# Modulation rows spread by DMA and copied into PSUM by ScalarE, in a fused residual stack on one core

## The reference, cut to what matters

```python
ctx = causal_ema(x, tau_ctx)
wg = sigmoid(concat([x, ctx]) @ Wg.T + bg)
gated = x * wg
h1 = gelu(x @ Wn1.T + bn1)
mod = 0.5 + sigmoid(h1 @ Wn2.T + bn2)            # [b, t, 16]
# for each of the 16 values of d:
traces[d] = causal_ema(gated * mod[..., d], tau_raws[d])
temporal = sum_d traces[d] * softmax(blend)[d]
gate = sigmoid(temporal @ Wtemp.T + btemp)
soma = gelu(x @ Wsoma.T + bsoma)
x = x + layernorm((soma * gate) @ Wout.T)
```

## Time and profile before

| | before |
|---|---|
| median of 3 runs | 2875.97 us |
| lowest, highest | 2873.36, 2878.23 us |
| profiled execution | 2876.17 us |
| its span, first to last instruction | 2874.4 us |
| granted TensorE clock, mean | 0.993 |
| busy: TensorE, VectorE, ScalarE, GpSimd | 2818.4, 1846.4, 1390.2, 1233.3 us |
| moved by DMA | 201.22 MB |

### The profile page before, as it was taken

One profiled execution on the slowest core, in us unless ns is written; L12 is line 12 of the kernel. 1 busy time (PEld: TensorE's weight loads), 2 busy tenths in 40 slices (PEclk: granted clock), 3 DMA queues, 4 the chain that ended last, 5 costly groups with the idle time before them and its releaser, 6 DMA issues.

```text
span 2874.4 us, 36550 instructions
## 1 busy us (share of the span) xinstructions
PE 2818.4 (98%) x13018; PEld 2331.4 (81%) x13018; DVE 1846.4 (64%) x3017; ACT 1390.2 (48%) x2408; POOL 1233.3 (43%) x950
## 2 busy tenths in 40 slices
PE   8699999999999999999999999999999999999999
PEld 5488888788888888888788888888888888888888
DVE  8699778867777766556865666655776563333443
ACT  4544555465336633454534553344643473333445
POOL 5256434643463445433554345542455333333333
PEclk9899999999999999999999999999999999999999
DMA  4133332322112311111311131111221122111231
GB/s 150 60 116 99 90 94 78 111 92 93 57 48 68 115 48 50 48 50 48 94 45 48 56 92 45 48 45 52 74 70 57 47 87 63 50 45 44 72 92 57
DMA packets 85573, 201.22 MB, mean 70 GB/s; under 512 B 10312, under 2 KB 27152, under 8 KB 85392
## 3 DMA queue, kind: packets, MB, share of 16 engines
q1 hardware_dynamic: 82256, 190.38, 21.5%
q0 software_dynamic: 2560, 8.39, 1.0%
q10 hardware_dynamic: 576, 0.11, 0.0%
HBM read 190.75 MB, written 8.09 MB: 69 GB/s over the span
## 4 chain that ended last, share of the span: by engine, by line
PE 88%; DVE 7%; issue 2%; ACT 2%; DMA 1%; SPq 0%; DVEq 0%; ACTq 0%
PE bank L557 19%; PE bank L559 19%; PE bank L558 19%; PE ps_out L557 9%; PE ps_out L559 9%; PE ps_out L558 9%; DVE trace L1075 2%; DVE w_lo L1145 2%; DVE trace L1067 1%; PE bank L550 1%; PE bank L631 1%; DVE hid L1169 0%; DMA stat<-mod_rows 0%; ACT L867 0%; PE bank L679 0%
## 5 line engine op out<-in xcount | busy, mean ns | idle before, releaser
L1308 POOL TENSOR_TENSOR hid_lo<-hid,hid_hi 128x512 fp32r<-128x512 f32 x640 | 865.6, 1353 | 1581.2 <-ACT hid_hi L954 1580.9
L557 PE MATMUL bank<-res_lo,w_hi 128*128 128x512 f32 x2432 | 963.3, 396 | 6.2 <-DVE res_lo L1160 3.3
L559 PE MATMUL bank<-res_hi,w_hi 128*128 128x512 f32 x2432 | 953.1, 392 | 0.0
L558 PE MATMUL bank<-res_hi,w_lo 128*128 128x512 f32 x2432 | 951.9, 391 | 0.0
L1169 DVE TENSOR_TENSOR hid<-hid,bank 128x512 f32<-128x512 f32 x576 | 393.3, 683 | 540.8 <-PE bank L559 512.8
L926 ACT ACTIVATE hid<-bank 128x512 f32<-128x512 f32 x576 | 344.0, 597 | 663.9 <-PE bank L559 662.8
L1145 DVE TENSOR_TENSOR w_lo<-w_raw,w_hi 128x768 fp32r<-128x768 f32 (+2 forms) x520 | 513.5, 989 | 177.9 <-ACT w_hi L895 139.6
L895 ACT ACTIVATE w_hi<-w_raw 128x768 fp32r<-128x768 f32 x392 | 331.4, 845 | 540.0 <-PE ps_out L559 513.4
L559 PEld LDWEIGHTS bank<-res_hi,w_hi 128*128 128x128 f32 x2432 | 458.3, 188 | 103.3
L557 PEld LDWEIGHTS bank<-res_lo,w_hi 128*128 128x128 f32 x2432 | 458.8, 189 | 100.5 <-issue 6.7
L558 PEld LDWEIGHTS bank<-res_hi,w_lo 128*128 128x128 f32 x2432 | 459.3, 189 | 86.4
(11 more groups left out here) (179 smaller groups left out, 1624.4 us busy)
## 6 DMA issues: line engine op xcount, KB each, us to landing
w_raw<-in_chunks SPq DMA_DIRECT2D x392, 384.0 KB
w_raw<-in_head_chunks SPq DMA_DIRECT2D x64, 224.0 KB
x_in<-in_xT SPq DMA_DIRECT2D x16, 256.0 KB, 3.6
pre_x<-in_xT SPq DMA_DIRECT2D x14, 256.0 KB, 7.0
soma_rows<-pre_soma SPq DMA_DIRECT2D x14, 256.0 KB, 2.0
soma<-soma_rows SPq DMA_DIRECT2D x14, 256.0 KB, 3.1
out_yT<-acc SPq DMA_DIRECT2D x7, 512.0 KB, 2.8
acc<-in_sidew SPq DMA_DIRECT2D x2, 512.0 KB, 7.1
```

The lines of the kernel that those rows point to most:

```text
L557: mm(out, wh, xl, start=start and i == 0, stop=False, skip_group_check=not lone)
L558: mm(out, wl, xh, start=False, stop=False, skip_group_check=not lone)
L559: last = mm(out, wh, xh, start=False, stop=end, skip_group_check=not lone)
L1308: nc.gpsimd.tensor_tensor(hid_lo[i % DEPTH][:], hid[i % 3][:], f(hid_hi[i % DEPTH][:]), ALU.subtract).then_inc(s_hlo, 1)
```

## The change

For blocks 1 to 7 no product makes the row. Instead, `spread` issues a DMA from ScalarE's queue that reads row d of `mod_rows` (256 numbers) and writes it to all 128 partitions of one of three tiles `mod_on` of the lane (the third is `stat`). `mix` waits for it and for the scan of d - 1 and writes it with an activation, 0.5 * row + 1, into the lane's PSUM bank, where VectorE reads it as before. Rows 0 and 1 of a block are issued at piece 25 of the block before, row 2 with row 0's copy, row d + 2 with row d's copy. The entry `mix` is placed into the list right behind the last `front` ahead of its piece, or behind the lane's piece before it if that comes later. The rows are no longer loaded on 16 partitions, and VectorE no longer scales and splits them. The wait for the stored soma moves from piece 5 to piece 28. Block 0 stays as it was. `mod_pair` now shares its place with `mod_on`.

```diff
--- before.py
+++ after.py
@@ -238,15 +238,30 @@
     out.append(("late", queue[-1]))
     while queue:
         back()
-    return out
+
+
+    placed, front, piece_of = [], 0, {}
+    for x in out:
+        if x[0] == "front":
+            front = len(placed)
+        elif x[0] == "side":
+            _, b, s, j = x
+            if b and 7 <= j < 7 + ND:
+                k = max(front + 1, piece_of[s] + 1)
+                placed.insert(k, ("mix", b, s, j - 7))
+                piece_of = {lane: p + (p >= k) for lane, p in piece_of.items()}
+                front = k if k == front + 1 else front
+            piece_of[s] = len(placed)
+        placed.append(x)
+    return placed
 
 
 
 
 SIDE_PE = (["h1", "soma", "mod", "gate"] + [f"mix{d}" for d in range(ND)]
            + ["tgate", "proj", "var", "attn", "score", "xT", "probT", "pooled"])
-SIDE_ACT = (["x_hi", "ctx_hi", "h1", "soma", "mod", "gate", "alpha",
-             "t_hi", "tgate", "p_hi", "sq", "q_hi", "cen", "std", "attn", "exp", "xT", "probT"])
+SIDE_ACT = (["x_hi", "ctx_hi", "h1", "soma", "mod", "gate", "alpha"] + [f"mix{d}" for d in range(ND)]
+            + ["t_hi", "tgate", "p_hi", "sq", "q_hi", "cen", "std", "attn", "exp", "xT", "probT"])
 SIDE_DVE = (["ctx", "x_lo", "ctx_lo", "mod", "mod_hi", "modpair", "gated"]
             + [f"{what}{d}" for d in range(ND) for what in ("mul", "scan")]
             + ["t_lo", "prod", "p_lo", "q_lo", "rstd", "norm", "affine", "x1", "score",
@@ -257,12 +272,15 @@
 
 def stages_in(stages, s, b):
 
-    if 1 <= b <= PRE and stages is not SIDE_DVE:
+
+    if b and stages is SIDE_ACT:
         return [x for x in stages if x not in ("h1", "soma", "mod")]
     if b:
-        return stages
+        return [x for x in stages if x not in ("h1", "soma", "mod", "mod_hi", "modpair") and not x.startswith("mix")]
 
     plain = [x for x in stages if x not in SPLITS and not (s and x == "alpha")]
+    if stages is SIDE_ACT:
+        plain = [x for x in plain if not x.startswith("mix")]
     if s == 0 and "soma" in plain:
 
         plain.remove("soma")
@@ -326,8 +344,17 @@
         trace = [[sb(f"trace{s}_{i}", [P, DH, S]) for i in range(3)] for s in range(BB)]
         soma = [sb(f"soma{s}", [P, DH, S]) for s in range(BB)]
         small = [sb(f"small{s}", [P, S]) for s in range(BB)]
-        mod_pair = [sb(f"mod_pair{s}", [P, S], f32r) for s in range(BB)]
         stat = [sb(f"stat{s}", [P, S]) for s in range(BB)]
+
+        pair_spots = []
+
+        def row_slot(s, i):
+            if i == 0:
+                pair_spots.append(-(-nc.sbuf_base // 32) * 32)
+            return sb(f"mod_on{s}_{i}", [P, S])
+
+        mod_on = [[row_slot(s, i) for i in range(2)] + [stat[s]] for s in range(BB)]
+        mod_pair = [nc.alloc_sbuf_tensor_at(f"mod_pair{s}", [P, S], f32r, offset=at_) for s, at_ in enumerate(pair_spots)]
         one_hi = [sb(f"one_hi{s}", [P, DH, S], f32r) for s in range(BB)]
         one_lo = [sb(f"one_lo{s}", [P, DH, S], f32r) for s in range(BB)]
         two_hi = [sb(f"two_hi{s}", [P, DH, S], f32r) for s in range(BB)]
@@ -412,6 +439,7 @@
         s_prex = [sem(f"pre_x_in{i}") for i in range(len(pre_x))]
         s_store = [sem(f"pre_out{i}") for i in range(3)]
         s_back = [sem(f"pre_back{s}") for s in range(BB)]
+        s_on = [[sem(f"mod_on{s}_{i}_in") for i in range(3)] for s in range(BB)]
         s_y = [sem(f"y_out{i}") for i in range(NACC)]
 
         su_dve, su_act, su_pe, su_pool = (sem(f"setup_{n}") for n in ("dve", "act", "pe", "pool"))
@@ -497,7 +525,6 @@
                 sp.wait_ge(l_dve[s], dve_at(s, b, "ctx"))
                 sp.wait_ge(s_store[u % 3], 32 * (u // 3 + 1))
                 sp.dma_start(soma[s][:].rearrange("p h t -> p (h t)"), soma_rows[u]).then_inc(s_back[s], 16)
-                sp.dma_start(stat[s][0:ND, :], mod_rows[u]).then_inc(s_back[s], 16)
 
             load_x(0, 0)
             for i in (2, 0):
@@ -616,16 +643,15 @@
                             pe.wait_ge(l_act[s], act_at(s, b, "mod"))
                         last = project(both, wg, b, one + two)
                     last.then_inc(l_pe[s], 1)
-                elif 7 <= j < 7 + ND:
+                elif b == 0 and 7 <= j < 7 + ND:
                     d = j - 7
                     if d == 0:
                         if not lead:
-                            pe.wait_ge(l_act[s], act_at(s, b, "alpha" if b else "gate"))
+                            pe.wait_ge(l_act[s], act_at(s, b, "gate"))
                         pe.wait_ge(l_dve[s], dve_at(s, b, "modpair"))
-                        if b == 0:
-                            pe.wait_ge(su_dve, su(SETUP_DVE, "small"))
+                        pe.wait_ge(su_dve, su(SETUP_DVE, "small"))
                     elif not lead:
-                        pe.wait_ge(l_dve[s], dve_at(s, b, f"scan{d - 1}" if b else f"mul{d - 1}"))
+                        pe.wait_ge(l_dve[s], dve_at(s, b, f"mul{d - 1}"))
                     elif d > 1:
                         pe.wait_ge(l_dve[s], dve_at(s, b, f"mul{d - 2}"))
                     mm((lead_mix[d % 2] if lead else ps)[:, 0:S], sel[:, d:d + 1].broadcast_to([P, P]), mod_pair[s][:],
@@ -840,6 +866,10 @@
                     act.wait_ge(l_act[s], act_at(s, b, "gate"))
                     activate(lead_alpha[:, 0:ND] if lead else ps[:, S:S + ND], alpha[:, 0:ND], ACT.Copy).then_inc(l_act[s], 1)
                 elif j == 25 and b:
+                    if b + 1 < NBLK:
+                        act.wait_ge(l_act[s], act_at(s, b, f"mix{ND - 1}"))
+                        spread(s, b + 1, 0)
+                        spread(s, b + 1, 1)
                     act.wait_ge(l_pool[s], pool_at(s, b, f"add{ND - 1}"))
                     activate(one_hi[s][:], temporal[s][:], ACT.Copy).then_inc(l_act[s], 1)
                 elif j == 27:
@@ -885,6 +915,26 @@
                     act.wait_ge(l_pe[s], pe_at(s, b, "probT"))
                     activate((soma if b == 0 else two_hi)[s][:], both, ACT.Copy).then_inc(l_act[s], 1)
 
+            def spread(s, b, d):
+
+                u = (b - 1) * BB + s
+                act.dma_start(mod_on[s][d % 3][:], mod_rows[u:u + 1, d, :].broadcast_to([P, S])).then_inc(s_on[s][d % 3], 16)
+
+            def mix(b, s, d):
+                k = d % 3
+                if d == 0:
+
+                    act.wait_ge(l_act[s], act_at(s, b, "alpha"))
+                    act.wait_ge(l_dve[s], dve_at(s, b - 1, "res"))
+                    spread(s, b, 2)
+                else:
+                    act.wait_ge(l_act[s], act_at(s, b, f"mix{d - 1}"))
+                    if d + 2 < ND:
+                        spread(s, b, d + 2)
+                    act.wait_ge(l_dve[s], dve_at(s, b, f"scan{d - 1}"))
+                act.wait_ge(s_on[s][k], 16 * ((ND // 3 + (k < ND % 3)) * (b - 1) + d // 3 + 1))
+                activate(ps_side[s][:, 0:S], mod_on[s][k][:], ACT.Copy, bias=1.0, scale=0.5).then_inc(l_act[s], 1)
+
             def cut(n):
                 e, b, c = CHUNKS[n]
                 k, raw = n % WSLOTS, w_raw[n % NRAW]
@@ -945,6 +995,9 @@
                 if i == 0:
                     for k in range(3):
                         act.wait_ge(s_store[k], 32 * len(range(k, NPRE, 3)))
+                    for s in range(BB):
+                        spread(s, 1, 0)
+                        spread(s, 1, 1)
                 if STEPS[i][0] == HEAD:
                     act.wait_ge(s_act, i + 1)
                 else:
@@ -974,6 +1027,8 @@
                     front(x[1])
                 elif x[0] == "late":
                     late(x[1])
+                elif x[0] == "mix":
+                    mix(*x[1:])
 
         @block.vector
         def _(dve):
@@ -1040,11 +1095,8 @@
                 elif j == 2 and b:
                     dve.wait_ge(l_act[s], act_at(s, b, "ctx_hi"))
                     TT(two_lo[s][:], cen[:], f(two_hi[s][:]), ALU.subtract).then_inc(l_dve[s], 1)
-                elif j == 5:
-                    if 1 <= b <= PRE:
-                        dve.wait_ge(s_back[s], 32 * b)
-                    else:
-                        dve.wait_ge(l_act[s], act_at(s, b, "mod"))
+                elif j == 5 and b == 0:
+                    dve.wait_ge(l_act[s], act_at(s, b, "mod"))
                     TS(mod, mod, 0.5, 1.0, ALU.mult, ALU.add).then_inc(l_dve[s], 1)
                     mine("mod")
                     V.tensor_copy(mod_pair[s][0:ND, :], mod).then_inc(l_dve[s], 1)
@@ -1062,14 +1114,17 @@
                         done("blend")
                     if d > 3:
                         dve.wait_ge(l_pool[s], pool_at(s, b, f"add{d - 3}"))
-                    dve.wait_ge(l_pe[s], pe_at(s, b, f"mix{d}"))
+                    if b:
+                        dve.wait_ge(l_act[s], act_at(s, b, f"mix{d}"))
+                    else:
+                        dve.wait_ge(l_pe[s], pe_at(s, b, f"mix{d}"))
                     for h in range(DH):
                         last = STT(tr[:, h, :], gated[s][:, h, :], bl[:, h, d:d + 1],
```

(6 more changed lines are left out.)

## The result

| | before | changed |
|---|---|---|
| median | 2876.93 us (4 runs) | 2839.49 us (4 runs, 2838.35 to 2840.43) |
| ratio | 1 | 0.9873, 95% interval 0.9858 to 0.9889 |
| span of the profiled execution | 2874.4 us | 2836.6 us |

The account below looks back on a forecast made before the run. The prediction took TensorE to bound the kernel. From 2876.2 us it subtracted 26.4 us for removed product slots and 5.4 us for removed waits, giving 2844.4 us, with a range of 2835 to 2859 us.

Parts of the forecast that it names:

- The bound: Over the whole span TensorE bounds the kernel, busy 98%; VectorE is second, at 82% and 78% in blocks 1 and 2.
- The slots: On TensorE in blocks 1 to 7, 224 one-hot products go, each giving back 0.118 us: 26.4 us.
- My own sign of a wrong price: A gain that divided by 224 isn't near 0.12 us would show a wrong price of TensorE's product slots.
- The removed waits: TensorE's waits before one-hot products, mostly at 520 and 878 us, plus low clock: half of 10.8 us returns, 5.4 us.
- VectorE and the place of the row: VectorE loses three instructions per lane and block and waits for rows: priced at nothing, up to 4 us of gain.
- ScalarE: 224 added copies of 0.40 to 0.50 us, issues up to 0.46 us and waits for scans, all covered: nothing.
- DMA: 224 added row loads take 7.5 points more of the DMA engines' time, the nearest load landing in 3.2 us: nothing.
- The rule on the shared port: VectorE and GpSimd lock a shared SBUF port pair; VectorE idle less often meets GpSimd more, speaking against the change.
- Rival (b): VectorE is locked out longer or more often, 5.1 us per case; two more cases give 2860 us; chance 0.06.
- (a): TensorE's slots come back, but waits only move and head runs lose some: 2850 to 2858 us; chance 0.13.
- (c): VectorE becomes the bound in blocks 1 and 2, whose 64 slots aren't given back: 2857 us; chance 0.05.
- (d): ScalarE's queue becomes the bound in blocks 1 to 3, 96 rows costing 44 us: 2894 us, slower; chance 0.06.

## Why the prediction was right, step by step

**The bound.** Right. TensorE's own products fill the span before and after, and freeing it paid.

**The slots.** The count (224) and the 118 ns were right, but the price was one term short. I read the distance to the next start and stopped there. The products behind started late for another 51 ns, 10.4 us in all by the table. It stood in the trace of before: the distances of 0.24 us behind the one-hot product at 1044.12 us. I had taken the median of all products, 227 ns, for what each of them takes. My own sign of a wrong price came up: the gain over 224 is 0.167 us, not near 0.12.

**The removed waits.** This step failed. I counted 5.4 us as coming back, half of 10.8 us. TensorE's waits over 290 ns were 27.2 us and are 27.6 us. The wait at 520 us became the two at 518 and 525 us, 3.9 us together, with the same cause upstream. The one at 878 us moved too, to a product that reads VectorE's `temporal`, with the low clock behind it as before:

```profile
873.71 1.25 PE L577 MATMUL bank<-temporal,wa 128*128 128x256 f32 x4 [1.96 <-DVE temporal L1159]
...
875.19 0.63 PE L585 MATMUL bank<-res_hi,w_lo 128*128 128x512 f32 x1
875.62 0.63 PE L586 MATMUL bank<-res_hi,w_hi 128*128 128x512 f32 x1
```

The low clock did fall a little in all (some 2 of the 4.8 us). The prediction had named the case in which the waits only move, and the cause that stays, and took half all the same, by how much TensorE could run ahead. The late engine was as late afterwards.

**VectorE and the place of the row.** I priced these at nothing, with up to 4 us of gain. Putting them back cost 4.5 and 10.9 us. These sizes are of kernels in which the products are gone: shorter steps of TensorE need VectorE sooner, so the relief was what kept the waits from growing by 12.2 us, as they did with the products alone changed. The step's premise, that none of VectorE's idle time is TensorE's, was wrong for the kernel that the change makes; for the kernel before no run isolates it.

**The sum.** 26.4 + 5.4 was near 37 because a missed term of 10 us stood beside a wrong one of 5. So the nearness of the sum is luck in part. The range held the time only because its low end had been left room for relieved waits: with the slots alone it would have ended at 2849.8 us.

**ScalarE.** Right. The copy took 383 ns, a little under the 0.40 to 0.50 us that I had; the issue 0.33 us in the median where I had up to 0.46 us, and it lay beside the Silu. The wait for the scan is 2.7 us in all. Twice as many copies on top changed nothing.

**DMA.** Right: landing 3.2 us; 4.3 points of the engines' time where I had 7.5.

**The rule on the shared port.** The Trainium skill ("SBUF — State Buffer", "SBUF: two separate sides") has a port pair that VectorE and GpSimd lock against each other for a whole instruction. The trace agrees that one holds up the other, and goes further than one instruction: 9.69 us for a subtraction under seven GpSimd instructions, gone when the chain is broken. What I made of it, that a VectorE relieved of waits meets GpSimd more often, did not come: the 392 subtractions of weight halves take 1110 ns in the mean where they took 1151, and GpSimd's additions of a trace 1340 ns where they took 1382. The longest was 9.7 us before and is 9.69 us after; one more of 2.9 us appeared at 172.6 us. Rival (b) did not occur; what it describes stays a cost of the kernel before as much as of the changed one.

**The other rivals.** Of (a) one half came true, the waits that only move, and the other, the loss at the head runs, did not. (c) did not occur; VectorE in the stretch of block 1 is busy 260.6 of 330.4 us, less than the 269.6 before. (d), the slower side, needed ScalarE's queue to fall behind; tripling its copies shows how far off that was. With the row still made by TensorE the early place did make the kernel 10 us slower.

## What to carry to other kernels

On the engine that bounds, price an instruction by the starts of the ten behind it, not by its own slot; and look for what those read when they are slower than the same instruction elsewhere. When the bound engine is relieved, its waits for the others don't vanish by themselves: here they stayed with the others relieved as well, and grew by 12.2 us without. Work that another engine waits for belongs early in the list, on an engine that can stand. And look at runs of short steps first when side work is spread over a list: keeping it out of them gave this kernel 17 us.

## What the runs showed of the hardware

- A product of 256 columns among products of 512 delays the next ten by 24 ns in sum, and one with a single column read as all 128 weight columns by 52 ns; a product of 512 columns by 3 ns. A wait ahead of it adds nothing (24 ns with and without). The Trainium skill, "TensorE: Matmul & The Clock Gate", section "Back-to-back issue gap", has the distance of two products set by weight load and product together, pipelined through a window. Whether that is what spreads this delay over ten products no run here shows.
- A VectorE subtraction with two inputs in SBUF, started while GpSimd worked without a pause, was held for all of its chain: 9.69 us, where the median is 0.95 us, beside seven GpSimd instructions.
- A DMA issue on ScalarE's queue took 0.33 us in the median of 224, and 0.41 to 0.48 us in 16 of them, spread over the run. The one at 306.17 us ran beside the activation ahead of it.
- After the wait of 3.66 us at 520 us TensorE's products started 0.44 us apart, the lower of its two clock levels, and 0.43 us apart after that of 1.96 us at 874 us in the changed kernel. After the waits of 2.42 us at 525 us and 1.96 us at 1639 us no product was as slow: the distances were 0.31 us once and then 0.23. In the stretch from 485 to 527 us the granted clock was 0.96 in the changed kernel and 1.00 in the one without side pieces in head steps.
